# A mixture-of-experts kernel: the narrow matmuls of neighbouring products put behind their wide ones

## The chip, the cores and the metric

One core of one Trainium2 chip runs the whole program. The metric is the device time of one execution in microseconds; the time before is the median of three runs.

## What is computed

A batch of 512 rows of 1024 features goes through eight experts (three dense layers each), whose outputs are mixed by two softmax gates and fed to two small towers. The reference, cut to what matters:

```python
h = jax.nn.relu(jnp.einsum('bi,eio->beo', x, eW1) + eb1)      # 8 experts, 1024 -> 1024
h = jax.nn.relu(jnp.einsum('beh,eho->beo', h, eW2) + eb2)     # 1024 -> 512
expert_out = jnp.einsum('beh,eho->beo', h, eW3) + eb3         # 512 -> 256
gates = jax.nn.softmax(jnp.einsum('bi,tie->bte', x, gW) + gb, axis=-1)
tin = jnp.einsum('bte,bed->btd', gates, expert_out)
th = jax.nn.relu(jnp.einsum('btd,tdh->bth', tin, tW1) + tb1)
th = jax.nn.relu(jnp.einsum('bth,tho->bto', th, tW2) + tb2)
out = jax.nn.sigmoid(jnp.einsum('bth,tho->bto', th, tW3) + tb3)
```

## The kernel before

Everything is held transposed, features on the 128 partitions and the batch in the free dimension. Each float32 operand is split into a high part (rounded to the matmul's type) and a low part (the rest), and a product is the sum of high by high, high by low and low by high. ScalarE makes the high part of weights (`..._hi`), VectorE subtracts it to make the low part (`..._lo`); VectorE's step is the later one and raises `slot_ready`.

Layer 1 of an expert is done in four *pairs* i = 0 to 3 of 128-row output groups by Strassen's scheme (Winograd's form): seven block products P1 to P7 instead of eight. Each block product is a 512-deep contraction, so four weight tiles (`KK` = 4) of 128 x 128. `product(e, p, i)` issues four *wide* matmuls (line 493: weights high; the moving operand is the high and low half side by side, 2 x 256 = 512 columns) and then four *narrow* ones (line 496: weights low by high half, 256 columns). The last narrow one raises `slot_used`, which tells ScalarE and VectorE that the product is done and its weight slot free. Products of x read `x_both`, the others `t_both`, sums of blocks of x made once.

On TensorE a pair runs P1, P2, P5, P6, P4 of the pair before, P3, P7 (`pair`, lines 501 to 541). Between them stand waits: P1 needs its weights from VectorE (`g1_lo`), P6 needs ScalarE to have copied P1's result out (`n1_take`), P4 needs VectorE's `c22_sum` of the pair before, P3 needs ScalarE's `p5_take`, P7 needs `n2_take`. P4 of pair 3 is `last_product`, behind layer 3 of the expert before (`layer3`), and then comes `layer2`: 96 wide matmuls (lines 348 to 350). Layer 3's second half waits for `upper_fold` of pair 3, for its bank.

The other engines each walk an order of their own, written out by hand, and stop at each instruction whose wait isn't met. VectorE's, around the change:

- `c22_sum(e, i)` (line 1097) subtracts P7's result of pair i; it waits for P7's last narrow matmul. Behind it in pair 0 stand `g2_lo` of pair 1 (line 1004), `hidden2_lo` (1020), `lower_fold` of pair 0 (1103), `c12_sum` (1075), `c11_sum` (1069), `g4_lo`, `upper_fold` (1090), `sum2` and `sum4` of pair 2 (1039, 1046) and `g1_lo` of pair 2 (1004 with 1536 columns), whose weights P1, P2 and P5 of pair 2 use. Then `c21_fold` of pair 0 (1109), `c12_sum` and `g2_lo`, and `c22_sum` of pair 1, and so on.
- `p5_take(e, i)` on ScalarE (line 809) waits for P5 and for `lower_fold` of the pair before. `c21_take` (line 820) waits for P4; VectorE's `c21_fold` follows it.

SP loads the blocks of the next pairs when the `slot_ready` of earlier ones is reached. The first expert (e = 0) runs outside the loop and does pairs 2 and 3 only, with its first four output groups in a plain form; between its two pairs stands `turn_logits`, four transposes that wait for ScalarE. Experts 1 to 7 run in a hardware loop.

Of the kernel before, what the change touches and what calls it, by code (L numbers as in the profile page):

```python
# [13 lines left out]
P = 128  # L14
# [6 lines left out]
HALF = BATCH // 2  # L21
# [29 lines left out]
PAIRS = H1 // P // 2  # L51
KK = KX // 2
# [30 lines left out]
FIRST_PAIR = 2  # L83
# [49 lines left out]
def nth(e, i):  # L133

    return PAIRS * (e - 1) + i + (PAIRS - FIRST_PAIR)
# [16 lines left out]
def splits(e):  # L152
    return SPLITS0 + (e - 1) * SPLITS


def split(e, *what):

    if isinstance(e, int) and e == 0:
        return PIECES + FIRST_SPLITS.index(what) + 1
    return splits(e) + SPLIT_ORDER.index(what) + 1  # L160


def slot_of(product):
    return USER[product] % RING


def moe_towers(nc, xT, eW1_first, eW1_pairs, eW2, eW3, tW1, tW2, small, out):
    with ExitStack() as ctx:
        def sb(name, shape, dt=F32):
            return ctx.enter_context(nc.sbuf_tensor(name, [P] + shape, dt))  # L170

        def sem(name):
            return ctx.enter_context(nc.semaphore(name))
# [7 lines left out]
        w_hi, w_lo = sb("w_hi", [RING, SLOT], F32R), sb("w_lo", [RING, SLOT], F32R)  # L181
# [10 lines left out]
        banks = [psum[:, b * BATCH:(b + 1) * BATCH] for b in range(8)]  # L192
# [42 lines left out]
        NX = len(X_SUMS)  # L235
# [7 lines left out]
        def halved(x):  # L243
            return x.rearrange("p (n b) -> p n b", n=2)
# [16 lines left out]
        t_ready = sem("t_ready")  # L261
# [4 lines left out]
        slot_ready = sem("slot_ready")  # L266
# [6 lines left out]
        n2_taken = sem("n2_taken")  # L273
# [4 lines left out]
        lower_summed = sem("lower_summed")  # L278
# [68 lines left out]
        def triple(pe, bank, weights_hi, weights_lo, moving_hi, moving_lo, first, last):  # L347
            pe.matmul(bank, weights_hi, moving_hi, start=first, stop=False)  # L348
            pe.matmul(bank, weights_hi, moving_lo, start=False, stop=False)  # L349
            return pe.matmul(bank, weights_lo, moving_hi, start=False, stop=last)  # L350
# [91 lines left out]
        def _(pe):  # L442
# [34 lines left out]
                        pe.matmul(banks[BANK_GROUP[m]][:], w[:, PIECE_SLOT[0], m * P:(m + 1) * P], x[:, 0, :],  # L477
                                  start=(n == 0), stop=False)

            def product(e, p, i):  # L480
                bank_of_pair, source, kh, xh, starts, ends = PRODUCTS[p]
                slot = slot_of((p, i))
                whole = halved(banks[bank_of_pair[i]])
                both = x_both if source == "x" else t_both

                def weights(w, kk):
                    return w[:, slot, kk * P:(kk + 1) * P]

                def moving(kk):
                    return both[:, :, kh * KK + kk, xh * HALF:(xh + 1) * HALF]  # L490

                for kk in range(KK):
                    pe.matmul(whole, weights(w_hi, kk), moving(kk), start=(starts and kk == 0), stop=False,  # L493
                              skip_group_check=True)
                for kk in range(KK):
                    mm = pe.matmul(whole[:, 0, :], weights(w_lo, kk), moving(kk)[:, 0, :], start=False,  # L496
                                   stop=(ends and kk == KK - 1), skip_group_check=True)
                mm.then_inc(slot_used, 1)

            def pair(e, i):  # L500
                first = isinstance(e, int)

                if i == PAIRS - 1 and not first:
                    pe.wait_ge(combined, nth(e, 0) + 1)
                elif i == 1:
                    pe.wait_ge(h2_staged, K3 * e)
                pe.wait_ge(slot_ready, split(e, "G0" if first else "G1", i))
                product(e, "P1", i)

                if not first and i >= 2:  # L510
                    pe.wait_ge(upper_done, nth(e, i) - 1)
                elif first and i == FIRST_PAIR:
                    pe.wait_ge(logitsT_ready, 1)
                elif first:
                    pe.wait_ge(h1_staged, 2)
                product(e, "P2", i)
                if first:
                    pe.wait_ge(slot_ready, split(e, "G1", i))
                    if i == FIRST_PAIR:
                        pe.wait_ge(t_ready, 1)  # L520
                if i == 0:

                    pe.wait_ge(gated_ready, 1 + GATED * (e - 1))
                product(e, "P5", i)

                pe.wait_ge(n1_taken, nth(e, i) + 1)
                pe.wait_ge(slot_ready, split(e, "G2", i))
                if first and i == FIRST_PAIR:
                    pe.wait_ge(t_ready, 2)
                product(e, "P6", i)  # L530
                if i > (FIRST_PAIR if first else 0):
                    last_product(e, i - 1)

                pe.wait_ge(p5_taken, nth(e, i) + 1)
                pe.wait_ge(slot_ready, split(e, "G3", i))
                product(e, "P3", i)

                pe.wait_ge(n2_taken, nth(e, i) + 1)
                if first and i == FIRST_PAIR:
                    pe.wait_ge(t_ready, NX)  # L540
                product(e, "P7", i)

            def last_product(e, i):

                pe.wait_ge(lower_summed, nth(e, i) + 1)
                pe.wait_ge(slot_ready, split(e, "G4", i))
                if isinstance(e, int):
                    pe.wait_ge(t_ready, NX)
                product(e, "P4", i)

            def layer2(e):
                first = isinstance(e, int)
                for n, m in by_tile(range(0, 6), MG) + by_bank(range(6, 8), MG):
                    k = ORDER2[n]
                    if first and (n, m) == (2, 0):
                        last_product(e, PAIRS - 1)
                        turn_gates()
# [81 lines left out]
            first_tile()  # L639
            first_group()  # L640
            pair(0, 2)
            turn_logits()
            pair(0, 3)
            layer2(0)
            with nc.Fori(1, E, engines=(PE,), hint_back_edge=True) as e:
                for i in range(PAIRS):
                    pair(e, i)
                layer3(e, last=False)
                last_product(e, PAIRS - 1)
                layer2(e)  # L650
# [4 lines left out]
            for t in range(T):  # L655
                pe.wait_ge(slot_ready, ready + t + 1)
                for i, (k, m) in enumerate((by_tile if t == 0 else by_bank)(range(KT1), KT2)):
# [5 lines left out]
                    if k == 0 and bank in BANK_OUT3:  # L663
                        pe.wait_ge(tail_gated, GATED)
                    slot, cols = 2 * t + k, slice(m * P, (m + 1) * P)
                    mm = triple(pe, banks[bank][:], w_hi[:, slot, cols], w_lo[:, slot, cols],
                                x_hi[:, t * OUT3 + k, :], x_lo[:, t * OUT3 + k, :], k == 0, k == KT1 - 1)
                    if k == KT1 - 1:
                        mm.then_inc(tower1_done, 1)
            def tower2_weights(t, k, m):  # L670
                slot = 2 * T + 2 * t + k // 2
                cols = slice((k % 2) * TH2 + m * P, (k % 2) * TH2 + (m + 1) * P)
                return w_hi[:, slot, cols], w_lo[:, slot, cols]

            for t in range(T):
                pe.wait_ge(slot_ready, ready + T + t + 1)
                for i, (k, m) in enumerate(by_bank(range(KT2), KT1)):
# [4 lines left out]
                    if k == 0:  # L682
                        pe.wait_ge(tower1_staged, 2 * t + m + 1)
                    mm = triple(pe, halved(banks[BANK_TOWER2[t][m]]), *tower2_weights(t, k, m),
                                h1_hi[:, :, t * KT2 + k, :], h1_lo[:, :, t * KT2 + k, :], k == 0, k == KT2 - 1)
# [3 lines left out]
            for h in range(2):  # L689
                pe.wait_ge(tower1_staged, 2 * t + m + 1 + h)  # L690
                for k in range(KT2):
                    mm = triple(pe, banks[BANK_LAST[h]][:, 0:HALF], *tower2_weights(t, k, m),
                                h1_hi[:, h, t * KT2 + k, :], h1_lo[:, h, t * KT2 + k, :], k == 0, k == KT2 - 1)
# [4 lines left out]
            for n, (t, cols) in enumerate([(0, slice(0, BATCH)), (1, slice(0, HALF)), (1, slice(HALF, BATCH))]):  # L698
                pe.wait_ge(folded, n + 1)
                pe.matmul(banks[BANK_FINAL[n]][0:1, cols], ones[:], tail_out[:, t * KT1, cols],  # L700
                          start=True, stop=True).then_inc(final_done, 1)
# [782 lines left out]
```

## Time and profile before

| | us |
|---|---|
| median of 3 runs | 573.57 |
| the runs | 573.57, 572.89, 573.98 |
| the profiled execution | 572.65 |
| its span, first to last instruction | 570.9 |

The granted TensorE clock was 1.00 on average. The profile's page gives busy time by engine. Its timeline shows instructions by start and length, with equal neighbours merged (x4), and in brackets the idle time of the engine before a row and what ended it. A matmul's shown length overlaps the next matmul (0.39 us for a wide one, though the next starts 0.23 us later), so paces are read from start to start. The same holds for VectorE and ScalarE: a 512-column operation is shown with 0.69 us and the next starts 0.60 us later. The first rows below are read for what share each engine is busy, the others for what stands when.

### The profile page before, as it was taken

What the parts mean: (1) busy time and instruction counts of PE and PEld (TensorE: products, weight loads), DVE (VectorE), ACT (ScalarE), POOL (GpSimd) and SP (SyncE); (2) the same over time, 40 slices, a digit from 0 to 9 for tenths busy, and PEclk for the clock granted to TensorE, in tenths of its full rate; (3) what the DMA queues carried; (4) which work ended last, traced back from release to release, by engine and by line L of the source; (5) the groups of instructions that cost most, each with busy time, mean ns of one, the idle gap of its engine ahead of it and who ended that gap; (6) DMA issues with size and microseconds to landing.
All of it is one profiled execution on the core that took longest, in us unless ns stands there. A gap on an engine that the chain in (4) does not pass through costs nothing.

```text
span 570.9 us, 8541 instructions
## 1 busy us (share of the span) xinstructions
PE 565.4 (99%) x2883; PEld 477.2 (84%) x2883; DVE 455.0 (80%) x576; ACT 310.8 (54%) x422; POOL 99.9 (18%) x106
## 2 busy tenths in 40 slices
PE   8999999999999999999999999999999999999998
PEld 6788888888888888888888888888888888888776
DVE  7998579975997769976899759977699768998493
ACT  3484566535763275724665356632757246654553
POOL 0201311052102411033200521024110332003000
DMA  9818675467726674467644577266644676426100
GB/s 324 227 51 233 155 224 130 156 164 173 170 82 190 174 179 110 147 166 201 175 121 162 149 183 167 89 198 175 173 100 147 165 210 168 118 73 211 47 1 0
DMA packets 39774, 86.87 MB, mean 152 GB/s; under 512 B 3521, under 2 KB 8769, under 8 KB 39762
## 3 DMA queue, kind: packets, MB, share of 16 engines
q1 hardware_dynamic: 29762, 66.50, 35.3%
q0 software_dynamic: 9856, 19.96, 20.1%
q10 hardware_dynamic: 144, 0.26, 0.2%
q8 instruction: 6, 0.10, 0.1%
q14 instruction: 6, 0.05, 0.0%
HBM read 86.68 MB, written 0.04 MB: 152 GB/s over the span
## 4 chain that ended last, share of the span: by engine, by line
PE 91%; DVE 3%; DMA 3%; ACT 1%; issue 1%; ACTq 0%; DVEq 0%
PE psum L493 33%; PE psum L496 17%; PE psum L348 14%; PE psum L349 14%; PE psum L350 14%; DMA w_raw<-eW_pairs 2%; DVE w_lo L1004 1%; DMA scratch<-xT 1%; DVE x_both L1135 0%; DVE t_both L1155 0%; DVE x_both L1133 0%; DVE scratch L1039 0%; ACT w_hi L959 0%; DVE scratch L1149 0%; ACT scratch L994 0%
## 5 line engine op out<-in xcount | busy, mean ns | idle before, releaser
L1004 DVE TENSOR_TENSOR w_lo<-w_raw,w_hi 128x1024 fp32r<-128x1024 f32 (+2 forms) x108 | 138.3, 1282 | 21.1 <-ACT w_hi L788 12.0
L348 PE MATMUL psum<-h_hi,w_hi 128*128 128x512 f32 (+1 forms) x340 | 131.9, 388 | 0.8 <-DVE h_lo L1020 0.8
L349 PE MATMUL psum<-h_lo,w_hi 128*128 128x512 f32 (+1 forms) x340 | 131.7, 387 | 0.0
L350 PE MATMUL psum<-h_hi,w_lo 128*128 128x512 f32 (+1 forms) x340 | 131.6, 387 | 0.0
L493 PE MATMUL psum<-t_both,w_hi 128*128 128x512 f32 x480 | 130.9, 394 | 0.0
L493 PE MATMUL psum<-x_both,w_hi 128*128 128x512 f32 x360 | 98.2, 394 | 0.0
L493 PEld LDWEIGHTS psum<-t_both,w_hi 128*128 128x128 f32 x480 | 82.6, 189 | 11.5
L1409 POOL DMA_DIRECT2D w_raw<-eW_pairs x30 | 25.9, 865 | 341.4 <-DMA w_raw<-eW_pairs 340.8
L1020 DVE SCALAR_TENSOR_TENSOR h_lo<-scratch,h_hi 128x512 fp32r<-128x512 f32 (+1 forms) x66 | 66.9, 1014 | 22.8 <-ACT scratch L851 19.5
L496 PEld LDWEIGHTS psum<-t_both,w_lo 128*128 128x128 f32 x480 | 73.7, 189 | 10.2
L1004 DVE TENSOR_TENSOR w_lo<-scratch,w_hi 128x512 fp32r<-128x512 f32 (+1 forms) x60 | 57.2, 954 | 24.6 <-ACT w_hi L781 24.0
L496 PE MATMUL psum<-t_both,w_lo 128*128 128x256 f32 x480 | 76.4, 281 | 0.0
L348 PEld LDWEIGHTS psum<-h_hi,w_hi 128*128 128x128 f32 x340 | 63.9, 188 | 13.7 <-DVE h_lo L1020 1.2
L350 PEld LDWEIGHTS psum<-h_hi,w_lo 128*128 128x128 f32 x340 | 63.9, 188 | 13.0
L349 PEld LDWEIGHTS psum<-h_lo,w_hi 128*128 128x128 f32 x340 | 64.0, 188 | 12.4
L493 PEld LDWEIGHTS psum<-x_both,w_hi 128*128 128x128 f32 x360 | 62.1, 189 | 8.7
L496 PEld LDWEIGHTS psum<-x_both,w_lo 128*128 128x128 f32 x360 | 55.3, 189 | 7.6
L496 PE MATMUL psum<-x_both,w_lo 128*128 128x256 f32 x360 | 57.3, 281 | 0.0
L1440 POOL TENSOR_TENSOR scratch<-scratch 128x512 f32<-128x512 f32 x28 | 41.7, 1500 | 73.8 <-DVE scratch L1128 73.8
L781 ACT ACTIVATE w_hi<-scratch 128x1024 fp32r<-128x1024 f32 x30 | 31.5, 1051 | 32.1 <-PE psum L350 32.1
L753 ACT ACTIVATE w_hi<-w_raw 128x1536 fp32r<-128x1536 f32 x28 | 41.5, 1481 | 13.1 <-PE psum L350 13.1
L825 ACT ACTIVATE h_hi<-scratch 128x1024 fp32r<-128x1024 f32 x30 | 31.8, 1061 | 21.5 <-DVE scratch L1109 21.5
(100 smaller groups left out, 582.4 us busy)
## 6 DMA issues: line engine op xcount, KB each, us to landing
w_raw<-eW_pairs SPq DMA_DIRECT2D x30, 768.0 KB, 4.2
w_raw<-eW SPq DMA_DIRECT2D x40, 512.0 KB, 4.0
scratch<-eW_pairs SPq DMA_DIRECT2D x30, 256.0 KB, 4.9
w_raw<-eW_pairs SPq DMA_DIRECT2D x30, 256.0 KB, 5.1
w_raw<-eW_pairs POOLq DMA_DIRECT2D x30, 256.0 KB, 5.0
scratch<-eW_pairs POOLq DMA_DIRECT2D x30, 256.0 KB, 6.5
scratch<-gates_dram POOLq DMA_DIRECT2D x8, 512.0 KB, 5.6
w_raw<-tW SPq DMA_DIRECT2D x4, 512.0 KB, 4.3
```

What stands on the lines that cost most here:

```text
L348: pe.matmul(bank, weights_hi, moving_hi, start=first, stop=False)
L349: pe.matmul(bank, weights_hi, moving_lo, start=False, stop=False)
L350: return pe.matmul(bank, weights_lo, moving_hi, start=False, stop=last)
L493: pe.matmul(whole, weights(w_hi, kk), moving(kk), start=(starts and kk == 0), stop=False, skip_group_check=True)
L496: mm = pe.matmul(whole[:, 0, :], weights(w_lo, kk), moving(kk)[:, 0, :], start=False, stop=(ends and kk == KK - 1), skip_group_check=True)
L753: act.activation(wide(slice(first, first + 3)), raw_block(i, A11, 3), ACT.Copy).then_inc(slot_hi, 1)
L781: act.activation(wide(slice(first, first + 2)), sums[:, at:at + 2, :].rearrange("p s w -> p (s w)"), ACT.Copy).then_inc(slot_hi, 1)
L825: act.activation(pair_of(h1_hi, i), quarter[:], ACT.Relu).then_inc(h1_taken, 1)
L1004: dve.tensor_tensor(wide(w_lo, slots), raw, wide(w_hi, slots).bitcast(F32), ALU.subtract).then_inc(slot_ready, 1)
L1020: return dve.scalar_tensor_tensor(lo, staged, 0.0, hi.bitcast(F32), ALU.max, ALU.subtract)
L1409: pool.dma_start(raw_block(i, A21), blocks_dram(e, i, A22), accum_op=ALU.add) \
L1440: pool.tensor_tensor(task_in[:, t * OUT3 + o, :], task_in[:, t * OUT3 + o, :], gated[:, n % 2, :], ALU.add).then_inc(added, 1)
```

## The change

`product` is cut in two: `high(p, i)` issues the four wide matmuls and `low(p, i)` the four narrow ones with the signal. A pair now begins with P7 of the pair before: wide ones of P7, P1 and P2 (12), then their narrow ones (12) in the same order. P5 and P6 stay as they were. Then P4 of the pair before and P3: 8 wide, 8 narrow. P7 of pair 3 and P4 of pair 3 stay on their own. The waits stand in front of the wide ones of the product that had them. The number of matmuls is the same, and the programs of the other engines are unchanged.

```diff
+            def high(p, i):
                 for kk in range(KK):
-                    pe.matmul(whole, weights(w_hi, kk), moving(kk), start=(starts and kk == 0), stop=False,
+                    whole, cols, moving, starts, _ = operands(p, i, kk)
+                    pe.matmul(whole, w_hi[:, slot_of((p, i)), cols], moving, start=(starts and kk == 0), stop=False,
                               skip_group_check=True)
+
+            def low(p, i):
                 for kk in range(KK):
...
                 mm.then_inc(slot_used, 1)
 
             def pair(e, i):
                 first = isinstance(e, int)
+                again = i > (FIRST_PAIR if first else 0)
+                if again:
+
+                    pe.wait_ge(n2_taken, nth(e, i))
+                    if first:
+                        pe.wait_ge(t_ready, NX)
+                    high("P7", i - 1)
...
-                product(e, "P1", i)
+                high("P1", i)
...
-                product(e, "P2", i)
+                high("P2", i)
+                if again:
+                    low("P7", i - 1)
+                low("P1", i)
+                low("P2", i)
...
-                product(e, "P6", i)
-                if i > (FIRST_PAIR if first else 0):
-                    last_product(e, i - 1)
+                product("P6", i)
+                if again:
+
+                    pe.wait_ge(lower_summed, nth(e, i))
+                    pe.wait_ge(slot_ready, split(e, "G4", i - 1))
+                    high("P4", i - 1)
 
                 pe.wait_ge(p5_taken, nth(e, i) + 1)
                 pe.wait_ge(slot_ready, split(e, "G3", i))
-                product(e, "P3", i)
-
-                pe.wait_ge(n2_taken, nth(e, i) + 1)
-                if first and i == FIRST_PAIR:
-                    pe.wait_ge(t_ready, NX)
-                product(e, "P7", i)
+                high("P3", i)
+                if again:
+                    low("P4", i - 1)
+                low("P3", i)
+                if i == PAIRS - 1:
+
+                    pe.wait_ge(n2_taken, nth(e, i) + 1)
+                    product("P7", i)
```

TensorE's order in the loop, where pair 1 ends and pair 2 begins; line 493 is a wide matmul and 496 a narrow one. Before, P7, P1 and P2:

```order
283 L493 MATMUL psum<-t_both,w_hi 128x512 [waits n2_taken]
284 L493 MATMUL psum<-t_both,w_hi 128x512 x3
285 L496 MATMUL psum<-t_both,w_lo 128x256 x4
286 L507 REGISTER_ALU
287 L493 MATMUL psum<-x_both,w_hi 128x512 [waits slot_ready]
288 L493 MATMUL psum<-x_both,w_hi 128x512 x3
289 L496 MATMUL psum<-x_both,w_lo 128x256 x4
290 L493 MATMUL psum<-x_both,w_hi 128x512 [waits upper_done]
291 L493 MATMUL psum<-x_both,w_hi 128x512 x3
292 L496 MATMUL psum<-x_both,w_lo 128x256 x4
```

And now, with line 490 the wide and 497 the narrow ones:

```order
277 L490 MATMUL psum<-t_both,w_hi 128x512 [waits n2_taken]
278 L490 MATMUL psum<-t_both,w_hi 128x512 x3
279 L519 REGISTER_ALU
280 L490 MATMUL psum<-x_both,w_hi 128x512 [waits slot_ready]
281 L490 MATMUL psum<-x_both,w_hi 128x512 x3
282 L490 MATMUL psum<-x_both,w_hi 128x512 [waits upper_done]
283 L490 MATMUL psum<-x_both,w_hi 128x512 x3
284 L497 MATMUL psum<-t_both,w_lo 128x256 x4
285 L497 MATMUL psum<-x_both,w_lo 128x256 x8
```

P7's four narrow ones (row 285 before) moved behind eight more wide ones, and P1's wait for `slot_ready` now stands in front of them.

TensorE's order in the first expert, from P3 of pair 2 on; the rows of `ident` are the transposes of the logits. Before:

```order
107 L493 MATMUL psum<-x_both,w_hi 128x512 [waits slot_ready,p5_taken]
108 L493 MATMUL psum<-x_both,w_hi 128x512 x3
109 L496 MATMUL psum<-x_both,w_lo 128x256 x4
110 L493 MATMUL psum<-t_both,w_hi 128x512 [waits t_ready,n2_taken]
111 L493 MATMUL psum<-t_both,w_hi 128x512 x3
112 L496 MATMUL psum<-t_both,w_lo 128x256 x4
113 L624 MATMUL psum<-ident,scratch 128x128 [waits h1_staged,logitsT_ready,ident_ready]
114 L624 MATMUL psum<-ident,scratch 128x128 x3
```

And now:

```order
106 L490 MATMUL psum<-x_both,w_hi 128x512 [waits slot_ready,p5_taken]
107 L490 MATMUL psum<-x_both,w_hi 128x512 x3
108 L497 MATMUL psum<-x_both,w_lo 128x256 x4
109 L645 MATMUL psum<-ident,scratch 128x128 [waits h1_staged,logitsT_ready,ident_ready]
110 L645 MATMUL psum<-ident,scratch 128x128 x3
111 L490 MATMUL psum<-t_both,w_hi 128x512 [waits t_ready,n2_taken]
112 L490 MATMUL psum<-t_both,w_hi 128x512 x3
```

P7 of pair 2 stood in front of the transposes and now stands behind them.

## Rows read from the trace of the kernel before

**Rows 1.** The page, part 1: engine, busy us, share, instructions.

```profile
PE 565.4 (99%) x2883; PEld 477.2 (84%) x2883; DVE 455.0 (80%) x576; ACT 310.8 (54%) x422; POOL 99.9 (18%) x106
```

**Rows 2.** Waits of TensorE, first of five: us in total, times, longest.

```profile
PE psum L638 <- DVE scratch L1158: 1.2, 1, 1.2
```

**Rows 3.** Timeline of TensorE, 200 to 212 us: start, us, engine, line, operation.

```profile
199.77 0.39 PE L350 MATMUL psum<-h_hi,w_lo 128*128 128x512 f32 x1
...
204.53 0.39 PE L350 MATMUL psum<-h_hi,w_lo 128*128 128x512 f32 x1
204.75 1.07 PE L493 MATMUL psum<-x_both,w_hi 128*128 128x512 f32 x4
205.66 0.64 PE L496 MATMUL psum<-x_both,w_lo 128*128 128x256 f32 x4
206.13 1.09 PE L493 MATMUL psum<-x_both,w_hi 128*128 128x512 f32 x4
207.06 0.63 PE L496 MATMUL psum<-x_both,w_lo 128*128 128x256 f32 x4
```

**Rows 4.** Timeline of TensorE, 204 to 246: P1 of pairs 1 to 3, P3, layer 3.

```profile
213.15 1.09 PE L493 MATMUL psum<-x_both,w_hi 128*128 128x512 f32 x4
...
222.97 1.09 PE L493 MATMUL psum<-x_both,w_hi 128*128 128x512 f32 x4
...
232.79 1.09 PE L493 MATMUL psum<-x_both,w_hi 128*128 128x512 f32 x4
...
239.81 1.09 PE L493 MATMUL psum<-x_both,w_hi 128*128 128x512 f32 x4
...
242.62 0.40 PE L348 MATMUL psum<-h_hi,w_hi 128*128 128x512 f32 x1
```

**Rows 5.** Timeline of VectorE, 200 to 270, the steps named in the text.

```profile
213.35 0.69 DVE L1097 TENSOR_TENSOR scratch<-scratch,psum 128x512 f32<-128x512 f32 x1 [0.80 <-PE psum L496]
...
219.60 1.75 DVE L1004 TENSOR_TENSOR w_lo<-w_raw,w_hi 128x1536 fp32r<-128x1536 f32 x1
...
223.18 0.69 DVE L1097 TENSOR_TENSOR scratch<-scratch,psum 128x512 f32<-128x512 f32 x1
...
230.47 1.75 DVE L1004 TENSOR_TENSOR w_lo<-w_raw,w_hi 128x1536 fp32r<-128x1536 f32 x1
...
233.07 0.68 DVE L1097 TENSOR_TENSOR scratch<-scratch,psum 128x512 f32<-128x512 f32 x1
...
238.06 0.48 DVE L1103 SCALAR_TENSOR_TENSOR scratch<-scratch,prm 128x256 f32<-128x256 f32 x1
...
240.70 0.42 DVE L1109 TENSOR_TENSOR scratch<-scratch,psum 128x256 f32<-128x256 f32 x1 [0.44 <-ACT scratch L820]
...
244.22 0.75 DVE L1090 SCALAR_TENSOR_TENSOR scratch<-scratch,prm 128x512 f32<-128x512 f32 x1
```

**Rows 6.** Timeline of ScalarE, 234 to 268: p5_take, c21_take, the last weight piece.

```profile
238.62 0.60 ACT L809 ACTIVATE scratch<-psum 128x512 f32<-128x512 f32 x1 [1.14 <-PE psum L496]
...
240.20 0.47 ACT L820 ACTIVATE scratch<-psum,prm 128x256 f32<-128x256 f32 x1 [0.48 <-PE psum L496]
...
254.31 1.06 ACT L840 ACTIVATE w_hi<-w_raw 128x1024 fp32r<-128x1024 f32 x1 [1.49 <-DMA w_raw<-eW]
```

**Rows 7.** Timeline of TensorE, 30 to 60: P7 of pair 2, the transposes.

```profile
35.99 1.09 PE L493 MATMUL psum<-t_both,w_hi 128*128 128x512 f32 x4
...
37.84 0.63 PE L624 MATMUL psum<-ident,scratch 128*128 128x128 f32 x4 [0.28 <-ACT scratch L721]
```

**Rows 8.** Timeline of VectorE, 30 to 60: c22_sum and lower_fold of pair 2.

```profile
38.91 0.69 DVE L1097 TENSOR_TENSOR scratch<-scratch,psum 128x512 f32<-128x512 f32 x1
...
43.11 0.49 DVE L1103 SCALAR_TENSOR_TENSOR scratch<-scratch,prm 128x256 f32<-128x256 f32 x1
```

**Rows 9.** A wait near the end, timeline of TensorE, 538.8 to 545.3.

```profile
540.24 0.50 PE L348 MATMUL psum<-h_hi,w_hi 128*128 128x512 f32 x1 [0.79 <-DVE h_lo L1020]
```

**Rows 10.** The stretch around it: us, busy PE, PEld, DVE, ACT, POOL, granted clock, DMA.

```profile
538.00:541.00 3.00, 2.21 (x10) 1.54 (x9) 2.50 (x4) 2.98 (x5) 0.00 (x0) 1.00 0.00 0
```

More of the change, by code:

```diff
@@ L478, in first_tile, with operands, product @@
                                   start=(n == 0), stop=False)
-            def product(e, p, i):
+            def operands(p, i, kk):
                 bank_of_pair, source, kh, xh, starts, ends = PRODUCTS[p]
-                slot = slot_of((p, i))
-                whole = halved(banks[bank_of_pair[i]])
                 both = x_both if source == "x" else t_both
[L486 to L490, printed above, removed]
+                return (halved(banks[bank_of_pair[i]]), slice(kk * P, (kk + 1) * P),
+                        both[:, :, kh * KK + kk, xh * HALF:(xh + 1) * HALF], starts, ends)
+            def high(p, i):
                 for kk in range(KK):
-                    pe.matmul(whole, weights(w_hi, kk), moving(kk), start=(starts and kk == 0), stop=False,
+                    whole, cols, moving, starts, _ = operands(p, i, kk)
+                    pe.matmul(whole, w_hi[:, slot_of((p, i)), cols], moving, start=(starts and kk == 0), stop=False,
                               skip_group_check=True)
+            def low(p, i):
                 for kk in range(KK):
-                    mm = pe.matmul(whole[:, 0, :], weights(w_lo, kk), moving(kk)[:, 0, :], start=False,
+                    whole, cols, moving, _, ends = operands(p, i, kk)
+                    mm = pe.matmul(whole[:, 0, :], w_lo[:, slot_of((p, i)), cols], moving[:, 0, :], start=False,
                                    stop=(ends and kk == KK - 1), skip_group_check=True)
                 mm.then_inc(slot_used, 1)
+            def product(p, i):
+                high(p, i)
+                low(p, i)
             def pair(e, i):
                 first = isinstance(e, int)
+                again = i > (FIRST_PAIR if first else 0)
[4 more added lines that the diff above has]
+                    high("P7", i - 1)
                 if i == PAIRS - 1 and not first:
@@ L523, in pair @@
                     pe.wait_ge(gated_ready, 1 + GATED * (e - 1))
-                product(e, "P5", i)
+                product("P5", i)
                 pe.wait_ge(n1_taken, nth(e, i) + 1)
@@ L548, in last_product @@
                     pe.wait_ge(t_ready, NX)
-                product(e, "P4", i)
+                product("P4", i)
             def layer2(e):
```

## The prediction

> **What bounds the kernel now.** I read the table of busy time first, then TensorE's waits, then the timelines of TensorE, VectorE and ScalarE over one expert, side by side. TensorE is busy 99% of the span and VectorE 80% [rows 1]. TensorE's five waits together are some 3 us, the longest 1.2 us, all before or after the expert loop [rows 2]. So the loop is a stream of matmuls without a gap, and the time is the sum of their paces plus whatever wait a new order brings.
>
> The pace: 21 wide matmuls of layer 2 take 204.53 - 199.77 = 4.76 us, 0.227 us each. The first product after them has its four wide ones in 0.91 us and its four narrow ones in 0.47; the four wide ones after those narrow ones take 0.93 [rows 3]. So each change from narrow to wide costs about 0.02 us. Seven products, a pair, take 222.97 - 213.15 = 9.82 us [rows 4].
>
> The timeline of VectorE is the warning. From the row of 213.35 to the one of 244.22 its instructions stand almost back to back [rows 5]; it walks a fixed order, and per pair it has about 9.9 us from one c22_sum to the next (223.18 to 233.07), of which only about half a microsecond is waiting, against TensorE's 9.82. An average of 80% hides that in the pairs VectorE keeps just ahead of TensorE, and that only through the slack of one ready weight group.
>
> **The change, part by part.** The diff touches TensorE's order alone; VectorE's, ScalarE's, SP's and GpSimd's programs stay.
>
> *Removed transitions.* Three products joined are two changes fewer, two joined are one: 3 per pair boundary, 3 boundaries per expert in the loop, one for the first expert: 22 x 3 = 66 changes. At 0.02 us that is 1.4 us saved. Bounds: nothing (the cost comes with the number of narrow ones), and 2 us at 0.03 us each. Long narrow runs I take at the 0.118 us of the short ones; the weight load of 0.19 us could at worst show, a rival below.
> The Trainium skill, TensorE: Matmul & The Clock Gate, section Back-to-back issue gap, gives a gap by width alone, N/2.4 + 2.5 ns (216 and 109 ns), by which order costs nothing and this saving would be zero; the rows have 227 and 118 ns and a price on the change, so the trace doesn't agree.
>
> *P7's narrow ones come later.* They stand behind the wide ones of the next P1 and P2: 8 x 0.227 = 1.8 us later than before. Their end lets VectorE do c22_sum, in front of which it now stands still and behind which everything else of VectorE is queued. I follow one expert, pair by pair, with TensorE 0.02 us quicker per removed change, 0.2 us from the end of a product to the engine that waits (213.15 to 213.35, [rows 4, 5]) and 0.1 us from VectorE's or ScalarE's end to TensorE, estimated from the rows of the one wait in the tail.
> - c22_sum of pair 0: 213.35 becomes 215.1. VectorE reaches the weights of pair 2 (219.60) 6.25 us behind it, of which 0.2 were waits that vanish: 221.1, done 222.9. TensorE wants them for P1 one wide quartet (0.93) after P7 begins, at 222.4; before it wanted them at 222.97 and they were done at 221.35. Stall 0.6 us.
> - P7's last narrow one of pair 1 then ends at 223.0 + 1.8 + 0.1 (the first weights after a stall are not prefetched) + 0.5 = 225.4, so c22_sum of pair 1 starts at 225.6 and not 223.18: 2.4 late. The weights of pair 3 came 7.29 us behind it (230.47), of which 0.5 us were waits that vanish: 232.4, done 234.15. TensorE wants them at 232.79 + 0.57 - 0.47 = 232.9. Stall 1.4 us.
> - c22_sum of pair 2 by the same steps: 234.3 + 1.8 + 0.1 + 0.5 + 0.2 = 236.9, not 233.07: 3.8 late. lower_fold of pair 2 (238.06) goes to 241.8, done at 242.3. ScalarE's p5_take of pair 3 already sat waiting for it (238.62, [rows 6]) and now starts at 242.3, done 242.9. TensorE's P3 of pair 3 waits for that: it stood at 239.81, would be due at 239.81 + 2.0 - 0.5 (P4's narrow ones now follow it) = 241.3, and starts at 243.0. Stall 1.7 us.
> - P4's narrow ones of pair 2 end behind P3's wide ones, at 244.5; c21_take (240.20) goes to 244.7 [rows 6] and c21_fold (240.70) to 245.2, 4.5 late. So upper_fold of pair 3 (244.22) is done at 249.5. Layer 3, moved from 242.62 to 246.4, needs it for its second bank after 12 matmuls, at 249.1. Stall 0.45 us.
> - Behind that TensorE has 5 us of layer 3 and P4 and 22 us of layer 2, which want VectorE's results by quarters, and the lag dies there. SP's loads, which wait for VectorE's weights, go late with it: the latest is the last piece of eW2, which ScalarE waits for at 254.31 [rows 6] and layer 2 wants after 72 of its 96 matmuls, 16.3 us after its start at 249.4, so over 9 us are left. At nothing.
> Sum per expert: 0.6 + 1.4 + 1.7 + 0.45 + 4 x 0.1 for restarts - 0.2 for 9 changes = 4.35 us; seven experts 30.5 us.
>
> *P4's narrow ones behind P3's wide ones*: 0.9 us later; its one consequence is in the fourth step. *P1's narrow ones*, 0.9 us later: n1_take has 1.9 us until P6 where it had 2.8, and takes 0.8 with its signal. At nothing.
>
> *The first expert.* The turning of the logits, which waited 0.28 us for ScalarE behind P7 of pair 2 (35.99 to 37.84, [rows 7]), now stands before P7: it waits from 35.99 to the same 37.84, so 1.4 us of work leave its cover. c22_sum (38.91, [rows 8]) goes to 41.7, lower_fold (43.11) to 45.9, and p5_take of pair 3 with it to 46.4, so that P3 starts at 47.1 and not 46.2: 0.9 us. Together 2.3 us.
>
> **Sum**: 30.5 + 2.3 = 32.8 us on the profiled execution's 572.65 us: 605.5; on the median of the runs, 573.57, which is 0.9 us above it: 606.4. I give 606.
>
> **Rivals.**
> *The cover holds* (not slower): VectorE's lag stays under the slack, stalls vanish and only the removed changes count: 573.57 - 1.4 = 572.2. For it: VectorE has 20% idle in all. Against: its idle time lies in layer 2, and the point at which it turns is a c22_sum late by 1.0 us plus 0.2 of vanishing waits (the weights of pair 2 done 221.35, now wanted 222.4); it is late by 1.8. The same case with no saving, the joining not doing what it says, is 573.6. Chance 0.05 together.
> *The lag does not build up*: VectorE makes up the lag between pairs, so each of three boundaries costs the first one's 0.7 and P3 of pair 3 nothing: 2.1 us per expert, 15 us + 2 = 590.5. For it: waits that vanish could be larger than what rows show (each row shows only the last). Chance 0.09.
> *Long narrow runs slow down to the weight load*: the record of a weight load is 0.19 us against 0.118 of pace. 60 joined narrow ones per expert at 0.07 us more are 4.2 us, less where they follow stalls: up to 30 us more, 636. Against: the four narrow ones of today already show one steady pace. Chance 0.03.
> *The clock*: four stalls of 0.6 to 1.7 us per expert might lower it. Where TensorE idled 0.79 us before, up to 540.24 [rows 9], the granted clock of the stretch around it is 1.00, the level of 2.4 GHz [rows 10]. If each stall took one block of 24 matmuls (4.2 us) to the 1.2 GHz level, that were 4 us x 28, past 700 us. The Trainium skill, same page, section HAM oscillation — how this bites in real kernels, lets idle gaps put the clock back to its half; the row speaks against that at this length. Chance 0.02.
>
> **How the numbers follow.** The forecast has 0.81. Its own bounds: with waits that vanish twice as large and signals at nothing the stalls are 0.3, 0.9, 1.2 and 0.1, 2.5 us, less 0.2, so 16 us + 1.5: 591; with slower signals (0.3 us) and nothing vanishing 0.9, 1.9, 2.2, 0.9 and restarts, 6.3 us, so 44 + 3: 620. Both ends at once are unlikely, since errors of one expert's steps partly cancel: 594 to 616 holds nine tenths of this case. With only that, 0.27 would be left out, so the low end reaches to the second rival, 588 to 616, and 0.18 is left out. A measurement tells 0.2% (1.1 us) from no change. Faster: 0.04; within 0.2%: 0.02; slower: 0.94.
>
> **What would show it.** In the new profile TensorE should have three kinds of waits in the loop, 7 times each: the first wide one of P1 on VectorE's weight difference (0.6 us in pair 2, 1.4 in pair 3), P3 of pair 3 on ScalarE's take, and layer 3's second half on VectorE; an expert should last 70.9 us instead of 66.5. VectorE should show a gap before c22_sum in every pair (2.6, 1.3 and 1.9 us). Twelve narrow ones in a row should keep 0.118 to 0.120 us. It is wrong if VectorE's c22_sum is late but the weights of pair 2 are ready at P1, or if the narrow runs change pace.

## The result

The changed kernel takes 612.53 us (median of six runs, 612.12 to 613.81) beside 573.50 us for the kernel before (six runs, 572.71 to 574.39): 1.0688 times as long, with a 95% interval of 1.0677 to 1.0700. The forecast was slower, 606.0 us in a range of 588 to 616. Its profiled execution has a span of 610.3 us, 39.4 us over the 570.9 of before. One expert, from its first P1 matmul to the next expert's, lasts 71.75 us where it lasted 66.50. Seven of those make 36.75 us, and the first expert's 2.7 us are the rest.

The page, part 1, of the changed kernel (columns as in [rows 1]), and the first part of its chain of work that ended last:

```profile
PE 576.6 (94%) x2883; PEld 474.7 (78%) x2883; DVE 450.8 (74%) x576; ACT 310.8 (51%) x422; POOL 99.9 (16%) x106
...
PE 59%; DVE 23%; issue 11%; DMA 3%; ACT 2%; DVEq 2%; ACTq 0%
```

VectorE now carries 23% of the chain, though it is busy for less time than before; it had 3% of it. TensorE's waits, the first five (us in total, times, longest), where [rows 2] had one of 1.2 us at the head:

```profile
PE psum L490 <- ACT scratch L830: 12.1, 8, 1.6
PE psum L490 <- DVE w_lo L1025: 11.8, 14, 1.1
PE psum L348 <- DVE scratch L1111: 2.9, 7, 0.4
PE psum L645 <- ACT scratch L742: 1.7, 1, 1.7
PE psum L659 <- DVE scratch L1179: 1.2, 1, 1.2
```

The first is ScalarE's p5_take (seven times P3 of pair 3, once in the first expert), the second VectorE's weight difference (P1 of pairs 2 and 3, seven each), the third upper_fold of pair 3 before layer 3's second half, the fourth the transposes of the first expert. These are the waits that the prediction named. The view shows them small, since it counts the idle time behind the modelled end of the matmul ahead. From start to start they are larger. TensorE's timeline over the expert that began at 204.75 before and at 217.98 now, 13.2 us later, which answers to [rows 4]:

```profile
223.58 1.18 PE L490 MATMUL psum<-x_both,w_hi 128*128 128x512 f32 x4
...
225.07 1.09 PE L490 MATMUL psum<-t_both,w_hi 128*128 128x512 f32 x4
226.17 2.12 PE L490 MATMUL psum<-x_both,w_hi 128*128 128x512 f32 x8
...
235.15 1.09 PE L490 MATMUL psum<-t_both,w_hi 128*128 128x512 f32 x4
236.85 2.10 PE L490 MATMUL psum<-x_both,w_hi 128*128 128x512 f32 x8 [0.61 <-DVE w_lo L1025]
...
245.84 1.17 PE L490 MATMUL psum<-t_both,w_hi 128*128 128x512 f32 x4
248.08 2.11 PE L490 MATMUL psum<-x_both,w_hi 128*128 128x512 f32 x8 [1.07 <-DVE w_lo L1025]
...
254.26 1.09 PE L490 MATMUL psum<-t_both,w_hi 128*128 128x512 f32 x4
256.97 1.18 PE L490 MATMUL psum<-x_both,w_hi 128*128 128x512 f32 x4 [1.61 <-ACT scratch L830]
...
262.87 0.39 PE L350 MATMUL psum<-h_hi,w_lo 128*128 128x512 f32 x1
263.67 0.50 PE L348 MATMUL psum<-h_hi,w_hi 128*128 128x512 f32 x1 [0.41 <-DVE scratch L1111]
```

Four wide matmuls take 0.93 us. So P1 of pair 2, behind the P7 row of 235.15, was due at 236.08 and came at 236.85: 0.8 us. P1 of pair 3 was due at 246.8 and came at 248.08: 1.3, of which 0.08 are a late second matmul of the P7 ahead of it (the row of 245.84 is 0.08 us longer than the one of 235.15). P3 of pair 3 (256.97) was due at 255.2: 1.8. Layer 3's second half (263.67) was due at 263.1: 0.6. P1 of pair 1 (226.17) came 0.17 late as well, which wasn't forecast. After each of these waits the next matmul follows after 0.33 to 0.34 us and not 0.23, the 0.1 us of restart; at 223.58, P3 of pair 0, there is such a restart without a wait to speak of.

VectorE over the same expert, which answers to [rows 5]: the three c22_sum (line 1118), the two late weight groups, lower_fold of pair 2, c21_fold of pair 2 and upper_fold of pair 3:

```profile
228.80 0.69 DVE L1118 TENSOR_TENSOR scratch<-scratch,psum 128x512 f32<-128x512 f32 x1 [2.24 <-PE psum L497]
...
235.05 1.75 DVE L1025 TENSOR_TENSOR w_lo<-w_raw,w_hi 128x1536 fp32r<-128x1536 f32 x1
...
239.47 0.69 DVE L1118 TENSOR_TENSOR scratch<-scratch,psum 128x512 f32<-128x512 f32 x1 [1.14 <-PE psum L497]
...
246.27 1.75 DVE L1025 TENSOR_TENSOR w_lo<-w_raw,w_hi 128x1536 fp32r<-128x1536 f32 x1
...
250.70 0.69 DVE L1118 TENSOR_TENSOR scratch<-scratch,psum 128x512 f32<-128x512 f32 x1 [1.74 <-PE psum L497]
...
255.67 0.48 DVE L1124 SCALAR_TENSOR_TENSOR scratch<-scratch,prm 128x256 f32<-128x256 f32 x1
...
259.34 0.42 DVE L1130 TENSOR_TENSOR scratch<-scratch,psum 128x256 f32<-128x256 f32 x1 [1.46 <-ACT scratch L841]
...
262.86 0.75 DVE L1111 SCALAR_TENSOR_TENSOR scratch<-scratch,prm 128x512 f32<-128x512 f32 x1
```

VectorE stands still 2.2, 1.1 and 1.7 us in front of c22_sum, where the forecast had 2.6, 1.3 and 1.9. It reaches the weights 6.25 us behind the first one (6.25 before) and 6.80 behind the second (7.29 before). ScalarE, which answers to [rows 6]: a copy of the hidden layer of the expert before (line 872), p5_take and c21_take:

```profile
225.33 0.71 ACT L872 ACTIVATE scratch<-psum,prm 128x512 f32<-128x512 f32 x1
...
256.24 0.60 ACT L830 ACTIVATE scratch<-psum 128x512 f32<-128x512 f32 x1 [2.05 <-DVE scratch L1124]
...
258.84 0.47 ACT L841 ACTIVATE scratch<-psum,prm 128x256 f32<-128x256 f32 x1 [1.51 <-PE psum L497]
```

p5_take of pair 3 is now plainly released by lower_fold (line 1124: 255.67, taken at 256.24). The first expert, TensorE, which answers to [rows 7]:

```profile
38.01 0.63 PE L645 MATMUL psum<-ident,scratch 128*128 128x128 f32 x4 [1.75 <-ACT scratch L742]
...
47.42 0.96 PE L490 MATMUL psum<-x_both,w_hi 128*128 128x512 f32 x3 [0.83 <-ACT scratch L830]
```

And the granted clock over the whole expert (us, busy PE, PEld, DVE, ACT, POOL, granted clock, DMA):

```profile
217.98:289.70 71.72, 68.01 (x345) 56.53 (x344) 52.91 (x65) 36.41 (x50) 13.03 (x13) 1.00 0.55 146
```

It stays at 1.00, the 2.4 GHz level, across waits of up to 1.8 us, and so does the clock of [rows 10].

### The profile page after: what moved, and what is told of

Its sections match the earlier page's. It is cut to its first block, busy times and chain, and to the rows that moved or that the text cites. A ratio compares the mean times of both kernels' runs of the same rounds, so it can differ in the third digit from the quotient of the medians.

```text
span 610.3 us, 8541 instructions
## 1 busy us (share of the span) xinstructions
PE 576.6 (94%) x2883; PEld 474.7 (78%) x2883; DVE 450.8 (74%) x576; ACT 310.8 (51%) x422; POOL 99.9 (16%) x106
## 3 DMA queue, kind: packets, MB, share of 16 engines
q1 hardware_dynamic: 29762, 66.50, 32.1%
## 4 chain that ended last, share of the span: by engine, by line
PE 59%; DVE 23%; issue 11%; DMA 3%; ACT 2%; DVEq 2%; ACTq 0%
PE psum L490 17%; PE psum L348 12%; PE psum L349 12%; PE psum L350 12%; DVE w_lo L1025 10%; PE psum L497 6%; DVE h_lo L1041 3%; DMA w_raw<-eW_pairs 2%; DVE scratch L1111 2%; DVE scratch L1096 2%; DVE scratch L1060 2%; DVE scratch L1124 1%; ACT scratch L830 1%; ACT scratch L841 1%; DMA scratch<-xT 1%
## 5 line engine op out<-in xcount | busy, mean ns | idle before, releaser
L1025 DVE TENSOR_TENSOR w_lo<-w_raw,w_hi 128x1024 fp32r<-128x1024 f32 (+2 forms) x108 | 136.0, 1263 | 25.2 <-ACT w_hi L809 15.5
L490 PE MATMUL psum<-x_both,w_hi 128*128 128x512 f32 x360 | 96.3, 402 | 23.9 <-ACT scratch L830 12.1
L490 PEld LDWEIGHTS psum<-x_both,w_hi 128*128 128x128 f32 x360 | 64.1, 188 | 49.8 <-DVE w_lo L1025 22.1
L350 PEld LDWEIGHTS psum<-h_hi,w_lo 128*128 128x128 f32 x340 | 63.9, 188 | 13.2
L497 PE MATMUL psum<-x_both,w_lo 128*128 128x256 f32 x360 | 52.8, 282 | 0.0
L497 PEld LDWEIGHTS psum<-x_both,w_lo 128*128 128x128 f32 x360 | 48.4, 191 | 1.3
L1118 DVE TENSOR_TENSOR scratch<-scratch,psum 128x512 f32<-128x512 f32 x30 | 20.6, 686 | 38.7 <-PE psum L497 38.6
```

Source lines behind the costliest of these rows:

```text
L490: pe.matmul(whole, w_hi[:, slot_of((p, i)), cols], moving, start=(starts and kk == 0), stop=False, skip_group_check=True)
L497: mm = pe.matmul(whole[:, 0, :], w_lo[:, slot_of((p, i)), cols], moving[:, 0, :], start=False, stop=(ends and kk == KK - 1), skip_group_ch ...
L1025: dve.tensor_tensor(wide(w_lo, slots), raw, wide(w_hi, slots).bitcast(F32), ALU.subtract).then_inc(slot_ready, 1)
L1118: dve.tensor_tensor(lower[:], lower[:], halved(banks[N_BANK[i]]), ALU.subtract).then_inc(lower_summed, 1)
```

## The experiments

The theory is that P7's narrow matmuls set VectorE's c22_sum, that VectorE stands still in front of it, and that all behind it, first the next weights, then lower_fold and with it ScalarE's p5_take, comes late. The first rival is that joining costs by itself, by its long runs or by P4 with P3, where the longest wait stands. Each ratio is against the kernel before, timed together with that run (its medians lie between 572.9 and 573.5 us).

| kernel | us | ratio (95%) | one expert, us |
|---|---|---|---|
| before | 572.9 to 573.5 | 1 | 66.50 |
| changed | 612.5 | 1.0688 (1.0677 to 1.0700) | 71.75 |
| P7 whole (e1) | 584.8 | 1.0210 (1.0192 to 1.0228) | 67.90 |
| P4, P3 apart (e2) | 603.6 | 1.0536 (1.0517 to 1.0554) | 70.53 |
| P7's narrow ones behind P1 (e3) | 593.1 | 1.0346 (1.0328 to 1.0364) | 69.04 |
| VectorE's order (e4) | 582.2 | 1.0160 (1.0142 to 1.0177) | 67.73 |
| only P1 with P2 (e5) | 575.0 | 1.0031 (1.0020 to 1.0042) | 66.73 |
| only P4 with P3 (e6) | 578.9 | 1.0098 (1.0083 to 1.0114) | 67.35 |
| P7, P1, P2 joined in pairs 1 to 3, VectorE's order (e7) | 574.8 | 1.0025 (1.0015 to 1.0036) | 66.69 |
| pair 0 apart (e9) | 610.7 | 1.0650 (1.0631 to 1.0669) | 71.41 |
| e7 with two edits more (e10) | 572.9 | 0.9993 (0.9984 to 1.0002) | 66.50 |
| e10 with P4, P3 joined in two pairs (e11) | 573.9 | 1.0011 (1.0002 to 1.0020) | 66.61 |

**P7 whole again (e1).** Against the changed kernel:

```diff
-                    high("P7", i - 1)
+                    product("P7", i - 1)
...
                 high("P2", i)
-                if again:
-                    low("P7", i - 1)
```

> One part undone: P7's narrow matmuls follow its own wide ones again, before P1 (P1 and P2 stay joined, P4 and P3 too). Theory (VectorE stands still in front of c22_sum, which waits for P7's last narrow one, and the weights queued behind it are late): c22_sum is early again, P1 of pairs 2 and 3 and P3 of pair 3 wait for nothing; what stays is P4's narrow ones 0.9 us late at layer 3's second half (0.5 us per expert), 0.1 us at P3 of pair 0 and 1.5 us in the first expert: about 579 us. Rival (the loss comes from joining as such: long narrow runs, emptied queues, P4 with P3): stays above 600 us.

584.83 us: 27.7 us of the 39 are gone with this one edit. TensorE's waits in the loop are now two, both seven times, and none of them on weights:

```profile
PE psum L348 <- DVE scratch L1109: 2.9, 7, 0.4
PE psum L490 <- ACT scratch L828: 2.7, 7, 0.4
```

The theory holds for P7 and the rival falls. The time is 6 us above the 579 expected: P3 of pair 3 still waits 0.55 us and 0.1 of restart, 4.5 us in seven experts.

**P4 and P3 apart, P7, P1 and P2 joined (e2).** 

```diff
-                    high("P4", i - 1)
+                    product("P4", i - 1)
...
-                high("P3", i)
-                if again:
-                    low("P4", i - 1)
-                low("P3", i)
+                product("P3", i)
```

> The other part undone: P4 and P3 are whole products again, P7, P1 and P2 stay joined 12 and 12. Theory: the waits of P1 of pairs 2 and 3 stay as they are (0.8 and 1.2 us), P3 of pair 3 still starts when ScalarE's take is done, so of 5.25 us per expert 0.5 us of narrow work and the 0.7 us at layer 3's second half come back: about 604 us. Rival (P4 with P3 carries the loss, since the longest wait stands at P3 of pair 3): under 590 us.

603.62 us. P1 of pairs 2 and 3 wait as before this edit (0.77 and 1.23 us from start to start), P3 of pair 3 waits 1.3 us instead of 1.8, and layer 3 not at all. The longest wait stood at P3, but P3 was not its cause: it waited for lower_fold, which was late with c22_sum.

**Half the dose (e3).** P7's narrow matmuls one product earlier:

```diff
                 high("P1", i)
+                if again:
+                    low("P7", i - 1)
...
                 high("P2", i)
-                if again:
-                    low("P7", i - 1)
```

> Half the dose: P7's narrow ones stand behind P1's wide ones, not behind P2's, so c22_sum is 0.9 us later than before the change and not 1.8. Theory: the weights of pairs 2 and 3 just meet their P1 (0 to 0.1 us of wait), lower_fold of pair 2 is 1.8 us late and P3 of pair 3 waits 1.3 us, layer 3 0.4 us: about 2.4 us per expert, 592 us. Rival (a lag under the slack costs nothing): 579 us as with P7 whole. Rival (cost in proportion to the lag from zero on): 595 us with waits of 0.4 us and more at P1 of pairs 2 and 3.

593.10 us, within 1.1 us of the theory's number, but in part by luck: P3 of pair 3 waits 0.87 us where 1.3 was expected, and P1 of pair 3, layer 3's second half (0.57) and P1 of pair 1 (0.17 us and 0.1 of restart, not counted on) make up for it. The lag of c22_sum of 0, 0.9 and 1.8 us makes an expert of 67.90, 69.04 and 71.75 us, so the second 0.9 costs 2.7 us where the first costs 1.1: the slack takes part of the first. TensorE's waits in the loop:

```profile
PE psum L490 <- ACT scratch L830: 4.9, 7, 0.7
PE psum L348 <- DVE scratch L1111: 2.9, 7, 0.4
PE psum L490 <- DVE w_lo L1025: 1.7, 7, 0.2
```

The weights are waited for seven times, not fourteen: P1 of pair 2 gets them in time, P1 of pair 3 waits 0.4 us. That is more than the 0.1 expected and less regular than the rival of proportion wanted.

**VectorE's order changed, TensorE's kept in the loop (e4).** In pair 0, for example:

```diff
-                c22_sum(e, 0)
                 g2_lo(e, 1)
                 hidden2_lo(e, 3)
+                c12_sum(e, 0)
+                upper_fold(e, 0)
+                c22_sum(e, 0)
                 lower_fold(e, 0)
-                c12_sum(e, 0)
                 c11_sum(e, 1)
                 g4_lo(e, 1)
-                upper_fold(e, 0)
```

> TensorE's order in the loop as in the changed kernel, VectorE's changed: in pairs 0, 1 and 2 c22_sum and lower_fold stand behind two to four steps that don't need P7 (g2_lo, hidden2_lo, c12_sum, upper_fold; pair_h1_lo, upper_fold; pair_h1_lo). The first expert keeps P7 of pair 2 in front of the transposes. Theory: VectorE fills the time in which it stood still, so the weights are in time and P3 of pair 3 too; what stays is P1 of pair 1 waiting for ScalarE (0.3 us), 0.1 us at P3 of pair 0 and up to 0.5 us at layer 3's second half: about 578 us. Rival (TensorE loses by its own order, whatever VectorE does): stays above 600 us.

582.24 us. This is the direct test: P7's narrow ones are as late as in the changed kernel, and when VectorE has something to do meanwhile an expert is 4.0 us shorter, 28 us in the loop (the first expert, with P7 back in its place, gives about 2 more). Its timeline around c22_sum of pair 0 (line 1116) and the weights of pair 2 (line 1023), the expert being 9.8 us ahead of the one shown for the changed kernel:

```profile
219.47 0.68 DVE L1116 TENSOR_TENSOR scratch<-scratch,psum 128x512 f32<-128x512 f32 x1
...
223.32 1.76 DVE L1023 TENSOR_TENSOR w_lo<-w_raw,w_hi 128x1536 fp32r<-128x1536 f32 x1
```

From c22_sum to the weights are 3.85 us and no longer 6.25, and no idle time stands in front of c22_sum. What is left in TensorE's waits, as the profile names them, is layer 3's second half, 0.57 us from start to start; P1 of pair 1 (0.17) and P1 of pair 3 (0.1) are too short to be named:

```profile
PE psum L348 <- DVE scratch L1109: 2.9, 7, 0.4
```

With their restarts and the one at P3 of pair 0 these make the 1.23 us by which an expert is still longer than before, and the run 4 us slower than expected. VectorE's new order beside TensorE's old one was not run, but in the kernel before TensorE waits for nothing in the loop (none of the waits that [rows 2] heads comes seven times), so that order had no wait of TensorE to take away there.

**Only P1 with P2 (e5)**, everything else as in the kernel before.

```diff
-                product(e, "P1", i)
+                high("P1", i)
...
-                product(e, "P2", i)
+                high("P2", i)
+                low("P1", i)
+                low("P2", i)
```

> One part alone: P1 and P2 joined 8 and 8 in every pair, P7, P4 and P3 whole and where they were. Theory: no narrow run delays c22_sum or c21_take; 30 changes fewer save 0.7 us, P3 of pair 0 costs 0.1 us per expert because P1's result is copied out later: 572.9 us, no change that can be told. Rival (every joining costs): 575 us or more.

575.02 us, slower by 0.2 to 0.4%: the rival. In the loop P3 of pair 0 restarts late, and P3 of pair 3 too: 0.23 us per expert, 1.6 of the 1.9 us. P1's narrow matmuls, 0.9 us later, do hold somebody: ScalarE, whose n1_take waits for them and whose further steps stand behind it.

In the first expert of the profiled execution P3 of pair 2 waits for p5_take, too, 0.52 us and 0.1 of restart. The join doesn't explain that one. e9 below has a wait of 0.47 us at the same place, though P1 and P2 of this pair are whole there. In both, a weight copy of ScalarE waits longer for its load. The copy before, in e5 and in e9:

```profile
24.82 0.63 ACT L766 ACTIVATE w_hi<-w_raw 128x512 fp32r<-128x512 f32 x1 [3.83 <-DMA w_raw<-eW_pairs]
...
26.51 0.63 ACT L780 ACTIVATE w_hi<-w_raw 128x512 fp32r<-128x512 f32 x1 [5.52 <-DMA w_raw<-eW_pairs]
...
26.62 0.63 ACT L788 ACTIVATE w_hi<-w_raw 128x512 fp32r<-128x512 f32 x1 [5.53 <-DMA w_raw<-eW_pairs]
```

p5_take follows 8.7 us behind it in all three (33.48, 35.17 and 35.29), while TensorE runs only 0.6 and 0.8 us later than before. So this wait comes with the time at which the first loads land.

**Only P4 with P3 (e6).** The edit, against the kernel before:

```diff
-                    last_product(e, i - 1)
+                    high("P4", i - 1)
...
-                product(e, "P3", i)
+                high("P3", i)
+                if again:
+                    low("P4", i - 1)
+                low("P3", i)
```

> One part alone: P4 and P3 joined 8 and 8, all else as before. Theory after the run with P7 whole: P3 of pair 3 waits 0.55 us and layer 3's second half 0.57 us, each with 0.1 us of restart, 1.3 us per expert, less 0.07 saved: 582 us. Rival (P3's wait in that run came from P1 with P2, not from P4's narrow ones): only layer 3's wait stays, 578 us.

578.88 us. Layer 3's second half waits 0.57 us and 0.1, P3 of pair 3 only 0.04 and 0.1: the rival's time. So the 0.55 us at P3 in the run with P7 whole needs both joins; alone P1 with P2 costs 0.23 us per expert and P4 with P3 0.85, together 1.40.

**Pair 0 apart (e9).** A pair 0 has no P7 ahead of it, and the change joins its P1 and P2 8 and 8; the same holds for pair 2 of the first expert. Here these are whole products again, the rest as in the changed kernel:

```diff
-                high("P1", i)
+                (high if again else product)("P1", i)
...
-                low("P1", i)
+                if again:
+                    low("P1", i)
```

> The changed kernel with P1 and P2 of pair 0 whole again, nothing else. Theory (the step that was priced at nothing: P1's narrow ones later hold ScalarE's n1_take and all that ScalarE has queued behind it, p5_take of pair 0 and the copies that P1 of pair 1 waits for): the late restart at P3 of pair 0 (0.1 us) and the wait at P1 of pair 1 (0.3 us) go, c22_sum of pair 0 is 0.4 us earlier, and an expert lasts 71.0 to 71.3 us instead of 71.75: 607 to 609 us. Rival (that wait comes from P1 of pair 1 being wanted 0.5 us earlier and stays): 612 us.

610.74 us, an expert of 71.41 us. The restart at P3 of pair 0 and the wait at P1 of pair 1 are gone from the trace. The gain is what they cost together, 0.35 us; the later waits only move forward with the rest and keep their size. The ratio falls from 1.0688 to 1.0650, which is 2.2 us, and seven experts make 2.4. The time is above the expected 607 to 609 since an expert was expected at 71.0 to 71.3.

**A version meant to keep the saving (e7).** TensorE joins P7, P1 and P2 in pairs 1 to 3 and nothing else in the loop, P1 and P2 in pair 3 of the first expert; pair 0 and P4, P3 are apart, VectorE has the order of e4, and P1 of pair 1 waits for two of ScalarE's copies and P2 for all four:

```diff
                 elif i == 1:
-                    pe.wait_ge(h2_staged, K3 * e)
+                    pe.wait_ge(h2_staged, K3 * (e - 1) + 2)
...
+                elif i == 1:
+                    pe.wait_ge(h2_staged, K3 * e)
                 high("P2", i)
```

> A version meant to keep the saving without the waits: P7, P1 and P2 joined 12 and 12 in pairs 1 to 3 of the loop, P4 and P3 apart, pair 0 apart, the first expert as before but for P1 with P2 of its pair 3, VectorE in the order with c22_sum later, and P1 of pair 1 waiting only for the two of ScalarE's copies that free its bank. Theory: no waits in the loop, 43 changes fewer at 0.022 us: 0.9 us, 572.6 us beside 573.5 before, at the edge of what can be told. Rival (narrow to wide changes cost nothing in sum, as the narrow ones of a long run are slower by what the wide ones gain): 573.5 us or more.

574.83 us, slower by 0.15 to 0.36%. An expert is 0.19 us longer, 1.3 of the 1.7 us, by short waits at P1 of pair 3 (0.05 us) and at layer 3's second half (0.05 and 0.1). In the profiled executions the second expert begins 1.24 us later than before (72.99 and 71.75), and the next expectation puts this down to P1 with P2 in the first expert. That is wrong. The matmuls of the logits, which stand ahead of every block product of that expert, already begin 1.24 us later, before and in e7:

```profile
21.53 1.92 PE L615 MATMUL psum<-scratch,gw 128*32 128x512 f32 x16
...
22.77 1.92 PE L634 MATMUL psum<-scratch,gw 128*32 128x512 f32 x16
```

From there to the second expert both take 50.2 us, so the join cost nothing there and the start-up differed.

**Two edits more (e10).** The first expert as before, which by e7's rows repairs nothing, and VectorE in pair 3:

```diff
-                c11_sum(e, 3)
                 w3_lo(e)
                 c21_fold(e, 2)
-                w2_lo(e, 0)
-                pair_h1_lo(e, 2)
+                c11_sum(e, 3)
                 c12_sum(e, 3)
+                pair_h1_lo(e, 2)
                 upper_fold(e, 3)
+                w2_lo(e, 0)
```

> The version before it with two repairs: the first expert in the old order entirely (the join of P1 and P2 there cost 1.2 us), and on VectorE in pair 3 c12_sum and upper_fold in front of the weights of layer 2, so that layer 3's second half doesn't wait. Theory (each narrow to wide change saves 0.022 us where nothing else waits): 42 changes fewer, 0.9 us, less 0.06 us per expert at P1 of pair 3: an expert of 66.4 us, 572.6 us beside 573.1 before. Rival (joining saves nothing): 573.1 us or more, an expert of 66.5 us.

572.87 us beside 573.06, a ratio of 0.9984 to 1.0002: no difference that can be told. An expert lasts 66.50 us as before, to the hundredth. The timeline of TensorE at the join of pair 1 shows what joining is worth:

```profile
212.12 1.09 PE L490 MATMUL psum<-t_both,w_hi 128*128 128x512 f32 x4
213.05 1.98 PE L490 MATMUL psum<-x_both,w_hi 128*128 128x512 f32 x8
214.87 0.64 PE L497 MATMUL psum<-t_both,w_lo 128*128 128x256 f32 x4
215.34 1.12 PE L497 MATMUL psum<-x_both,w_lo 128*128 128x256 f32 x8
216.30 0.86 PE L490 MATMUL psum<-t_both,w_hi 128*128 128x512 f32 x3
```

Twelve wide and twelve narrow take 216.30 - 212.12 = 4.18 us, and three whole products took 4.21 (3 x 1.403 by [rows 4]): 0.03 us for two changes fewer. Matmul by matmul, the wide ones behind a narrow run come at 234, 236, 228, 232 and 231 ns and then 227; the long narrow run goes at 120 ns, the short ones at 118.5 on average. The first gives 0.04 us for two changes, the second takes back 0.01. Three joins make nearly 0.09 us an expert. A late start in P1 of pair 3 (0.05), slower wide matmuls behind it (0.02) and nine slowed matmuls instead of five at the start of layer 3 (0.02) use that up.

**P4 with P3 in pairs 1 and 2 (e11).** The same kernel, with

```diff
-                product("P3", i)
+                if again and not first and i < PAIRS - 1:
+                    high("P3", i)
+                    low("P4", i - 1)
+                    low("P3", i)
+                else:
+                    product("P3", i)
```

and P4 in front of it by its wide ones alone.

> The same, with P4 and P3 joined in pairs 1 and 2 of the loop, apart in pair 3. Theory: P4's narrow ones 0.9 us late delay ScalarE's c21_take and, with VectorE's order as it is, c21_fold of pairs 0 and 1; VectorE has 0.1 to 0.5 us to spare per pair there, so P1 of pairs 2 and 3 wait up to 0.4 us: 573 to 576 us. Rival (only pair 3's join costs, by layer 3): 572.3 us.

573.87 us, 0.02 to 0.20% above the kernel before. An expert lasts 0.1 us more than in e10, most of it a late restart at P1 of pair 3.

## Why the prediction was right, and by how much it was off

**The mechanism and its order** are as predicted, shown by e1 (P7's place alone is worth 27.7 us), by the dose in e3 and by e4, where VectorE's order alone takes back 28 us. All four waits per expert stand where they were put.

**The terms of one expert** (predicted sum 4.35 us, measured 5.25), waits from start to start:

| step | predicted, us | measured, us |
|---|---|---|
| P3 of pair 0, P1 of pair 1 (P1's narrow ones later) | nothing | 0.1 restart; 0.17 + 0.1 |
| P1 of pair 2 | 0.6 | 0.8 |
| P1 of pair 3, with P7 before it | 1.4 | 1.3 |
| P3 of pair 3 | 1.7 | 1.8 |
| layer 3's second half | 0.45 | 0.57 |
| restarts of these four | 0.4 | 0.43 |
| changes saved | -0.2 | at most -0.1 |

The step that failed is the one that priced P1's narrow matmuls at nothing. It looked at P6, the product that waits for n1_take, and there the 1.9 us of slack do hold. It missed what ScalarE has queued behind n1_take: the weights of pair 1, p5_take of pair 0 and the last of the four copies of the hidden layer, which P1 of pair 1 waits for (at 225.33 in the timeline above and at 211.63 before, so 13.7 us later, where the expert itself is 13.2 later). That P1 is also wanted 0.4 us earlier, since P7's narrow matmuls no longer stand in front of it; e9 keeps this and has no wait there, so it is not enough by itself. e9 measures the step: 0.35 us an expert, 2.4 us of the 6.5 by which the forecast was short. e5 shows it without P7, in the loop.

The second error is the 0.2 us of waits that were to vanish before the weights of pair 2. The distance stayed 6.25 us. The idle times inside it are VectorE waiting for its own step before (0.17 us in front of lower_fold), and such a wait moves with its cause. In the next pair 0.5 us did vanish, a wait for ScalarE (7.29 to 6.80 us). That is why pair 3 came out right and pair 2 didn't.

**The saving** was taken at about 0.02 us a change and is 0.015 in a join of three products and 0.005 to 0.015 in joins of two; the longer pace of long narrow runs had been set to nothing. The count was off as well: P1 and P2 are joined in a pair without a P7 ahead, too, which makes 74 changes and not 66, 10 an expert and not 9. In sum this is about half a us.

**The first expert** was 2.3 us in the forecast and is 2.7: the transposes start at 38.01, not at 37.84, and P3 of pair 3 waits 1.0 us and 0.1 of restart where 0.9 was expected. The difference is at the edge of what one execution tells: from the logits to the second expert e10 takes 50.5 us and e11, with the same programs there, 50.2.

**The rivals.** That the cover holds fell: the point at which it turns (1.2 us) fits e3, where the lag is smaller and pair 2 doesn't wait. That the lag doesn't build up fell: 0.8, 1.3, 1.8 us. By the timelines it builds up as each wait of TensorE pushes the next P7 back. In e4, where VectorE has work in front of c22_sum, the waits at P1 of pair 2 and P3 of pair 3 are gone and 0.1 us is left at P1 of pair 3. Long narrow runs keep 0.120 us per matmul and don't fall to the 0.19 us of a weight load. The clock stayed at the level of 2.4 GHz.

## What to carry to other kernels

Where one engine hands work to engines that walk a fixed order, a later signal costs everything queued behind its wait, and the busy share of that engine doesn't tell the price; count from the waiting instruction to the next thing that the bound engine needs, on each engine that takes the signal. Of the idle times on that way only those for another engine can vanish, while a wait for the engine's own step stays. Change the consumer's order together with the producer's: that alone was worth 28 of 39 us here, and without waits the regrouping itself was worth less than could be measured.

## What the runs showed of the hardware

Wide matmuls behind narrow ones are slower for a while: in e10's join they come at 234, 236, 228, 232 and 231 ns and then at 227. In e1 all eight of P1 and P2 of pair 1 are slow (235, 233, 236, 224, 231, 236, 228 and 233 ns). A narrow one in a long run takes 120 ns, the first behind wide ones 113 to 118. So the net of one change fewer is 0.015 us in e10's join of three products. In e1 a join of two takes 2.802 us (P1 with P2) or 2.793 (P4 with P3), where two whole products take 2.807. Why the slow stretch has two lengths stays open.

After each wait of TensorE in the loop of the changed kernel, of 0.17 us or of 1.8, the second matmul comes 0.1 us late. At P3 of pair 0 the same appears behind a wait of only 0.02 us. That there the signal comes just as the matmul is due is argued from ScalarE's timeline, not tested.
